# An attention and mixture-of-experts block on one core: VectorE's output sum and its statistics become two steps, one head apart

## The chip, the core and the metric

The kernel is one program on one core of a Trainium2 chip. Its time is device time in microseconds (us), from one launch. TensorE is called PE here, its weight loads PEld, VectorE DVE, ScalarE ACT, GpSimd POOL and SyncE SP, as in the profile.

## The reference

```python
# x: 8 batches x 256 tokens x 256 features
x = x + _layernorm(attn(_layernorm(x)))     # latent attention, 16 heads of 16, softmax over 256 keys, output product wo, bias bo
x = x + _layernorm(ffn(_layernorm(x)))      # 8 experts, top 1, and a shared expert
...
scores = jnp.einsum('bqhd,bkhd->bhqk', q, k) / np.sqrt(hd)
probs = jax.nn.softmax(scores, axis=-1)
a = jnp.einsum('bhqk,bkhd->bqhd', probs, v).reshape(bs, sl, nh * hd)
return _lin(a, wo, bo)
```

`_layernorm` subtracts the mean over the 256 features and divides by the square root of the variance plus 1e-5. The part that the change touches is the tail of the attention of one batch: the sum of the output product and its bias, its normalization, the sum with x, and the statistics of the second normalization, the one before the experts.

## The kernel before

The batches go through eight slots of 16 heads each. Every engine has its own hand-written program, in which a table called `order` says what is done behind which head; engines meet only at semaphores. In slot b the heads of batch b are computed: at head h PE makes the transposed scores (L1623), ACT takes their exponential (L884), and behind every fourth head PE multiplies a group of four heads with v (L1603). Beside that run steps of other batches. A step named with SM, `sm_scores` and `sm_max`, belongs to batch b+1: PE makes the scores of a pair of heads (L1564) into one of two banks in turn, and DVE takes their negated maximum per query (`nmax`, L1098). PE may start the pair u only when the maxima up to u-2 are done, because there are only two banks. Steps with A work on batch b+2, with B on batch b+3, and the tail of the attention (D) on batch b-1 and its second part (E) on b-2. Within a head the maximum comes first and the listed steps behind it.

The D steps form a chain over two engines. DVE adds product and bias (`d_wo`, L1118, semaphore `y_ready`), takes mean and variance (`bn_stats`, `bn_aggr`, L1002, L1006, and L1122 for `var_at`). POOL raises the variance to the power -1/2 (D_power, L644, `rstd_at`). DVE normalizes (D_yn, L1128, two instructions). POOL adds x (D_x1, L684, `x1_ready`). DVE takes the statistics of that sum (D_stats, `stats_ff`, ending in L1136, `var_ff`). POOL takes the power again (D_power2, L644, `rstd`). In the next slot, behind the second head, DVE normalizes for the experts (E_xn2, L1145), and PE transposes that behind the fourth head (E_xn2T, L1430).

POOL has one more task at the beginning of a slot. P_M1 (`m_split`, L672 to L678, four small instructions) splits the second half of the maxima of the slot's own batch into three bfloat16 parts. It stands in POOL's program directly behind D_power2. PE turns the parts behind the third head (M1, L1584), and everything on PE behind M1 waits in line: the products for the keys and queries (L1502), the next heads, and E_xn2T. The rotary step of DVE (A_T, L1054) stands before E_xn2 and is waited for by the products at L1502. A primed name below (u0', h2') is a pair or head of the next slot; heads are counted from 0.

The last slot has lists of its own. In slot 7 the steps for batch 6 and the ones for batch 7 follow each other without maxima between them. The tail of batch 5 ends there: E_xn2 comes behind head 0 on DVE, E_xn2T behind head 2 on PE; behind head 3 comes D_avT0 (L1430), which needs a copy by ACT (D_o1, L877).

Semaphores order all of it:

```python
pe.wait_ge(sm["sm_max"], NH if (b, u) == (1, 0) else NH * b + u - 1)   # PE, a pair of scores
pe.wait_ge(sm["m_parts"], 8 * b + 4 * half + 4)                        # PE, M0 and M1
order = {0: ("P_M1",), 2: ("B_power",), 8: ("A_kres", "M0",),          # POOL
         9: ("A_qres",), 10: ("A_klow",), 11: ("A_qlow",), 12: ("D_power",), 13: ("D_x1",),
         15: ("D_power2",)}
```

Of the kernel before, what the change touches and what calls it, by code (L numbers as in the profile page):

```python
# [116 lines left out]
def program(nc, x, const, w_down, w_q, w_kv, w_rope, w_out, w_router, bias_col, bias_v, bias_o,  # L117
# [6 lines left out]
    with ExitStack() as ctx:  # L124
# [145 lines left out]
        def two(t):  # L270
            return t[:, :].rearrange("p (a c) -> p a c", a=2)
# [39 lines left out]
        def counted(value):  # L311

            return not isinstance(value, int) or value > 0
# [65 lines left out]
        def play(steps, text):  # L379

            for word in text.split():
                name, n = word.split(":")
                steps[name](int(n), int(n) % 2)
# [18 lines left out]
        def run_attention(eng, head, steps, order, last, behind=lambda *_: None):  # L402

            for n, names in PROLOGUE:
                for name in names.split():
                    if name[0] == "S":
                        steps["SM"](0, 0, int(name[1:]))  # L410
                    elif name in steps:
                        steps[name](n, n % 2)
            for b in range(B):
                run_slot(b, b % 2, head, steps, order, last, behind)

        def nothing(*_):
            return None
# [551 lines left out]
        def _(dve):  # L969
# [29 lines left out]
            def ln_head(name, b, tiles, stat, mean_var, var_ap, n):  # L999

                for t in range(n):
                    dve.bn_stats(stat[:, t, :], tiles(t)).then_inc(sm[f"{name}_stats"], 1)  # L1002
                dve.wait_ge(sm[f"{name}_stats"], n * (b + 1))
                dve.sem_inc(sm["passed"], 1)
                for t in range(n):
                    dve.bn_aggr(mean_var(t), stat[:, t, :]).then_inc(sm[f"{name}_aggr"], 1)  # L1006
                dve.wait_ge(sm[f"{name}_aggr"], n * (b + 1))
# [49 lines left out]
            def third_q(m):  # L1057

                def f(b, par):
                    if b != 2:  # L1060
                        return
                    dve.wait_ge(sm["qk_ps"], 3)
                    dve.wait_ge(sm["ql"], 2)
                    dve.wait_ge(sm["q_sb"], 4)
                    dve.tensor_scalar(qf[:, m, :], two(w1)[:, m, :], bcol[:, 2 + m:3 + m], None, ALU.add
                                      ).then_inc(sm["q_sb"], 1)
                return f

            def first_k(m):
                def f(b, par):  # L1070
                    dve.wait_ge(sm["hqk_ps"], 1)
                    for dst, col in ((kh_even, C_EVEN), (kh_odd, C_ODD)):
                        dve.scalar_tensor_tensor(dst[:, m, :], two(st_bank[0])[:, m, :], bcol[:, 14 + m:15 + m],
                                                 cst[:, col:col + 1].to_broadcast([P, S]), ALU.add, ALU.mult
                                                 ).then_inc(sm["hk_sb"], 1)
                return f
# [24 lines left out]
            def divide(t):  # L1101
                def f(b, par):
                    dve.wait_ge(sm["avT_ps"], 2 * b + t + 1)
                    o = w2[:, :].rearrange("p (h c) -> p h c", c=2 * HD)
                    dve.reciprocal(rec[:, :], o[:, :, HD]).then_inc(sm["rec_ready"], 1)
                    dve.wait_ge(sm["rec_ready"], 2 * b + t + 1)
                    if counted(b):
                        dve.wait_ge(sm["aT_ps"], b)
                    dve.tensor_tensor(a_sb[:, t, :].rearrange("p (h c) -> p h c", c=HD), o[:, :, 0:HD],
                                      rec[:, :].unsqueeze(2).to_broadcast([P, NH, HD]), ALU.mult  # L1110
                                      ).then_inc(sm["a_ready"], 1)
                return f

            def d_wo(b, par):
                dve.wait_ge(sm["wo_ps"], b + 1)
                if counted(b):
                    dve.wait_ge(sm["x1_ready"], b)
                dve.tensor_tensor(y_sb[:, :, :], two(w2), bo_sb[:, :].unsqueeze(1).to_broadcast([P, TB, D]),  # L1118
                                  ALU.add).then_inc(sm["y_ready"], 1)
                dve.wait_ge(sm["y_ready"], b + 1)  # L1120
                ln_head("at", b, lambda t: y_sb[:, t, :], stats["at"], lambda t: mv["at"][:, t, :], None, TB)
                dve.tensor_scalar(var["at"][:, :], mv["at"][:, :, 1], EPS, None, ALU.add  # L1122
                                  ).then_inc(sm["at_var"], 1)
# [25 lines left out]
            def d_router(b, par):  # L1149
# [4 lines left out]
            steps = {  # L1154
                "O_rows": ones, "A_ones": ones_and_sums, "A_kv": keys_sum, "A_T": rope, "A_ev0": third_q(0), "A_ev1": third_q(1),
                "H_k0": first_k(0), "H_k1": first_k(1), "B_stats": a_stats, "B_norm": a_norm, "F_stats": first_stats, "F_norm": first_norm, "N_v": v_add, "SM": sm_max,
                "D_div0": divide(0), "D_div1": divide(1), "D_y": d_wo, "D_yn": d_yn, "D_stats": d_stats,
                "E_xn2": d_xn2, "E_router": d_router}
            order = {1: ("A_T", "E_xn2"), 2: ("B_stats",), 3: ("B_norm",), 5: ("E_router",),
                     6: ("D_div0",), 8: ("D_div1",), 9: ("N_v",), 11: ("D_y",),  # L1160
                     12: ("D_yn",), 14: ("D_stats",)}


            done = [0]
# [145 lines left out]
            def unit_copy(seq, n, side):  # L1310
# [3 lines left out]
            steps.update({"O": one_hots, "g": gains, "c": scaled, "p": ranks_of_tokens, "l": low_one_hots,  # L1314
                          "n": expert_places, "m": tile_one_hots, "r": tile_rows, "e": tile_experts, "q": way_back,
                          "h": hidden})
            last = {0: "E_xn2:5", 3: "D_div0:6 D_div1:6", 6: "E_router:5 O:0 D_y:6 D_yn:6 p:0 g:0 c:0 c:1 D_stats:6 c:2 c:3",
                    13: "E_xn2:6"}

            def tile_first(seq, p):  # L1320
# [2 lines left out]

            steps["w"] = tile_first
            run_attention(dve, nothing, steps, order, last)
            play(steps, "D_div0:7 c:4 c:5 E_router:6 D_div1:7 h:0 c:6 c:7 c:8 c:9 D_y:7 h:1 D_yn:7 D_stats:7 h:2 E_xn2:7"
                        " E_router:7 O:1 c:10 c:11 h:3 g:1 c:12 c:13 c:14 c:15 p:1 n:0 h:4 m:0 h:5 l:0 l:1 l:2 l:3 e:0 h:6 r:0 q:0"
                        " h:7 w:8 w:9 h:8")

# [627 lines left out]
```

## Time and profile before

| | |
|---|---|
| time, median of 3 runs | 426.26 us (424.71 to 427.06) |
| the profiled execution | 424.66 us, its span 422.8 us |
| PE busy, of the span | 399.0 us, 94% |
| PEld | 300.2 us, 71% |
| DVE | 272.9 us, 65% |
| ACT | 207.3 us, 49% |
| POOL | 130.6 us, 31% |

The busy shares are means over the whole span. Slots 1 to 4 take 23.4 us each; the times at which an instruction starts, and what ended the idle time before it, are given by the timeline. The end of a PE instruction is modelled, so its start is the safer number.

### The profile page before, as it was taken

What the parts mean: (1) busy time and instruction counts of PE and PEld (TensorE: products, weight loads), DVE (VectorE), ACT (ScalarE), POOL (GpSimd) and SP (SyncE); (2) the same over time, 40 slices, a digit from 0 to 9 for tenths busy, and PEclk for the clock granted to TensorE, in tenths of its full rate; (3) what the DMA queues carried; (4) which work ended last, traced back from release to release, by engine and by line L of the source; (5) the groups of instructions that cost most, each with busy time, mean ns of one, the idle gap of its engine ahead of it and who ended that gap; (6) DMA issues with size and microseconds to landing.
All of it is one profiled execution on the core that took longest, in us unless ns stands there. A gap on an engine that the chain in (4) does not pass through costs nothing.

```text
span 422.8 us, 9481 instructions
## 1 busy us (share of the span) xinstructions
PE 399.0 (94%) x3411; PEld 300.2 (71%) x3411; DVE 272.9 (65%) x632; ACT 207.3 (49%) x381; POOL 130.6 (31%) x185
## 2 busy tenths in 40 slices
PE   8998999999999999797989999999999999999991
PEld 8765557676767776463768999999994444588991
DVE  5665677978878777865675694222226898725876
ACT  1745748585776667545551213344447767311110
POOL 2424515344251615303402002221112220026873
PEclk9999999999999999998999999999999999999998
DMA  7845235373635546450147750011111111124342
GB/s 251 212 119 150 58 94 184 91 225 95 220 85 163 150 111 193 102 175 12 43 144 229 224 177 26 27 50 51 52 50 51 40 47 32 51 59 123 106 127 74
DMA packets 50772, 47.29 MB, mean 112 GB/s; under 512 B 5350, under 2 KB 45542, under 8 KB 50726
## 3 DMA queue, kind: packets, MB, share of 16 engines
q1 hardware_dynamic: 44795, 38.31, 30.8%
q0 software_dynamic: 1632, 4.46, 3.8%
q10 hardware_dynamic: 4299, 3.92, 2.8%
q8 instruction: 28, 0.46, 0.5%
q14 instruction: 18, 0.15, 0.1%
HBM read 25.19 MB, written 8.65 MB: 80 GB/s over the span
## 4 chain that ended last, share of the span: by engine, by line
PE 73%; DVE 13%; issue 4%; POOL 3%; ACT 3%; DMA 2%; another core or an unknown queue 1%; DVEq 0%; ACTq 0%; POOLq 0%
PE bank L1426 32%; PE bank L1754 7%; PE bank L1430 6%; PE bank L1603 6%; PE bank L1623 6%; PE bank L1564 5%; PE bank L1779 3%; DVE nmax L1098 2%; PE bank L1502 2%; PE bank L1439 2%; PE bank L1550 2%; PE bank L1492 1%; DVE wall L1128 1%; DVE stacks L1396 1%; DVE stats_at L1002 1%
## 5 line engine op out<-in xcount | busy, mean ns | idle before, releaser
L1098 DVE TENSOR_REDUCE nmax<-bank 128x2 f32<-128x512 f32 x112 | 74.2, 686 | 27.3 <-PE bank L1564 26.7
L1426 PE MATMUL bank<-stacks,wall 128*128 128x128 f32 x512 | 61.9, 276 | 0.9 <-ACT stacks L920 0.4
L1426 PEld LDWEIGHTS bank<-stacks,wall 128*128 128x128 f32 x512 | 60.0, 192 | 3.5 <-issue 2.4
L1304 DVE TENSOR_TENSOR stacks<-stacks,bank 128x512 f32<-128x512 f32 x34 | 23.3, 686 | 51.9 <-PE bank L1426 47.3
L884 ACT ACTIVATE pv<-bank 128x512 f32<-128x512 f32 x64 | 38.3, 603 | 35.2 <-PE bank L1623 34.3
L920 ACT ACTIVATE stacks<-bank 128x512 f32<-128x512 f32 x34 | 20.3, 597 | 65.3 <-PE bank L1426 38.9
L884 ACT ACTIVATE wall<-bank 128x512 f32<-128x512 f32 x64 | 38.3, 606 | 25.2 <-PE bank L1623 25.1
L1623 PE MATMUL bank<-stacks 99*128 99x256 bf16 x256 | 49.2, 276 | 1.4 <-ACT wall L884 0.9
L1426 PE MATMUL bank<-wall,stacks 128*128 128x256 f32 (+1 forms) x208 | 49.5, 381 | 0.8 <-DVE stacks L1304 0.8
L1564 PE MATMUL bank<-stacks 96*128 96x256 bf16 x224 | 42.3, 273 | 6.6 <-DVE nmax L1098 6.5
L716 POOL DMA_INDIRECT stacks<-x_sc,row_i x18 | 20.3, 1126 | 89.2 <-PE bank L1430 70.1
L1426 PEld LDWEIGHTS bank<-wall,stacks 128*128 128x128 f32 x208 | 37.5, 190 | 5.3 <-DVE stacks L1304 1.2
L1623 PEld LDWEIGHTS bank<-stacks 99*128 99x128 bf16 x256 | 21.6, 100 | 23.5 <-issue 12.4
L1426 PEld LDWEIGHTS bank<-stacks,pv 128*128 128x128 f32 x320 | 37.2, 192 | 1.2 <-ACT stacks L914 0.7
L1426 PE MATMUL bank<-stacks,pv 128*128 128x128 f32 x320 | 37.4, 275 | 0.5 <-ACT stacks L914 0.5
L1754 PE MATMUL bank<-wall,stacks 128*32 x64 | 30.1, 595 | 0.5 <-ACT wdo_sb L933 0.5
L1564 PEld LDWEIGHTS bank<-stacks 96*128 96x128 bf16 x224 | 20.3, 97 | 13.9 <-DVE nmax L1098 11.3
L656 POOL TENSOR_TENSOR wall<-wall,low_sb 128x512 f32<-128x512 f32 x14 | 16.1, 1159 | 38.2 <-ACT low_sb L850 38.2
L731 POOL DMA_INDIRECT pv<-y_exp,back_i x16 | 16.0, 1001 | 33.8 <-DMA y_exp<-stacks 29.7
L1430 PE MATMUL bank<-cst,wall 128*128 128x128 f32 x160 | 24.0, 276 | 1.1 <-ACT wall L877 0.5
L1430 PEld LDWEIGHTS bank<-cst,wall 128*128 128x128 f32 x160 | 17.8, 140 | 4.7 <-issue 1.5
L1312 DVE COPY pv<-wall 128x1024 f32 x24 | 16.7, 695 | 4.3 <-PE bank L1779 1.7
(213 smaller groups left out, 798.4 us busy)
## 6 DMA issues: line engine op xcount, KB each, us to landing
stacks<-low_sb SPq DMA_DIRECT2D x144, 64.0 KB, 2.0
wall<-gate_up SPq DMA_DIRECT2D x8, 1024.0 KB, 5.4
wall<-down SPq DMA_DIRECT2D x8, 512.0 KB, 6.7
y_exp<-stacks ACTq DMA_DIRECT2D x18, 128.0 KB, 1.7
x_tok<-wall SPq DMA_DIRECT2D x8, 256.0 KB, 2.5
stacks<-x_tok SPq DMA_DIRECT2D x16, 128.0 KB
out<-stacks SPq DMA_DIRECT2D x8, 256.0 KB
stacks<-low_sb SPq DMA_DIRECT2D x12, 128.0 KB, 2.4
```

Of the source, the lines that this page charges most:

```text
L716: pool.indirect_dma_start(out=xl[:, par, :], out_offset=None, in_=x_sc, in_offset=bass.IndirectOffsetOnAxis(ap=row_i[:, s - R0:s - R0 + 1] ...
L884: act.activation(probs[h // QUAD % 2][:, h % QUAD, :], st_bank[h % 2][:, :], ACT.Exp, scale=SCALE).then_inc(sm["exp_done"], 1)
L920: act.activation(sg, fg[:, :], ACT.Silu).then_inc(sm["sg_sb"], 1)
L1098: dve.tensor_reduce(nmax[:, half, qt, 2 * pair:2 * pair + 2], two(sm_bank[u % 2]), AX.X, ALU.max, negate=True).then_inc(sm["sm_max"], 1)
L1304: dve.tensor_tensor(to, sg, fu[:, :], ALU.mult).then_inc(sm["h_sb"], 1)
L1312: dve.tensor_copy(to, of).then_inc(sm[("gate_dve", "up_dve", "down_dve")[side]], 1)
L1426: last = pe.matmul(out_ap, lhsT, rhs, start=(n == 0), stop=(n == len(pairs) - 1))
L1430: return pe.transpose(out_ap, in_ap, ident)
L1564: last = pe.matmul(two(sm_bank[u % 2])[:, c, :], stacks[0:ROWS, par, 0, place(h), P * qt:P * qt + P], stacks[0:ROWS, par, 1, place(h), :], ...
L1603: last = pe.matmul(two(av_bank)[32 * c:32 * c + 32, g % 2, :], v_aug[:, par, k, QUAD * g + c, :], probs[g % 2][:, c, S * k:S * k + S], sta ...
L1623: last = pe.matmul(two(st_bank[h % 2])[:, k, :], stacks[0:MROWS, par, 1, place(h), P * k:P * k + P], stacks[0:MROWS, par, 0, place(h), :], ...
L1754: last = pe.matmul((fg, fu)[r][U * n:U * n + U, :], xT[:, p, P * k + U * n:P * k + U * n + U], w, start=(k == 0), stop=(k == KT - 1))
```

## The change

`d_wo` is split: the sum with the bias stays behind head 11 (the twelfth), and the statistics of it become a step of their own, `d_ystats` or D_ys, behind head 12. The normalization D_yn moves from head 12 to 13 and the second statistics D_stats from head 14 to 15. In the lists of slot 7 and behind it, D_ys stands directly behind D_y, so the order of work there is the same as before.

```diff
             def d_wo(b, par):
...
                 dve.tensor_tensor(y_sb[:, :, :], two(w2), bo_sb[:, :].unsqueeze(1).to_broadcast([P, TB, D]),
                                   ALU.add).then_inc(sm["y_ready"], 1)
+
+            def d_ystats(b, par):
                 dve.wait_ge(sm["y_ready"], b + 1)
                 ln_head("at", b, lambda t: y_sb[:, t, :], stats["at"], lambda t: mv["at"][:, t, :], None, TB)
                 dve.tensor_scalar(var["at"][:, :], mv["at"][:, :, 1], EPS, None, ALU.add
...
-                     6: ("D_div0",), 8: ("D_div1",), 9: ("N_v",), 11: ("D_y",),
-                     12: ("D_yn",), 14: ("D_stats",)}
+                     6: ("D_div0",), 8: ("D_div1",), 9: ("N_v",), 11: ("D_y",), 12: ("D_ys",),
+                     13: ("D_yn",), 15: ("D_stats",)}
```

This is DVE's program from the output sum in slot 2 to the beginning of slot 3, before the change (BN_STATS of `stats_at` and `stats_ff` are the two statistics, `nmax` the maxima):

```order
L1118 TENSOR_TENSOR wall<-bank,bo_sb 128x512
L1002 BN_STATS stats_at<-wall 128x6 x2
L1006 BN_AGGR mv_at<-stats_at 128x2 x2
L1122 TENSOR_SCALAR var_at<-mv_at 128x2
L1098 TENSOR_REDUCE nmax<-bank 128x2
L1128 SCALAR_TENSOR_TENSOR wall<-wall,mv_at,rstd_at 128x256 x2
L1098 TENSOR_REDUCE nmax<-bank 128x2 x2
L1002 BN_STATS stats_ff<-x_sb 128x6 x2
L1006 BN_AGGR mv<-stats_ff 128x2 x2
L1136 TENSOR_SCALAR var_ff<-mv 128x2
L1098 TENSOR_REDUCE nmax<-bank 128x2 x3
L1054 SCALAR_TENSOR_TENSOR rope_t<-bank,bcol,cst 128x256
```

And the same place with the change, whose line numbers behind L1118 are higher by two:

```order
L1118 TENSOR_TENSOR wall<-bank,bo_sb 128x512
L1098 TENSOR_REDUCE nmax<-bank 128x2
L1002 BN_STATS stats_at<-wall 128x6 x2
L1006 BN_AGGR mv_at<-stats_at 128x2 x2
L1124 TENSOR_SCALAR var_at<-mv_at 128x2
L1098 TENSOR_REDUCE nmax<-bank 128x2
L1130 SCALAR_TENSOR_TENSOR wall<-wall,mv_at,rstd_at 128x256 x2
L1098 TENSOR_REDUCE nmax<-bank 128x2 x2
L1002 BN_STATS stats_ff<-x_sb 128x6 x2
L1006 BN_AGGR mv<-stats_ff 128x2 x2
L1138 TENSOR_SCALAR var_ff<-mv 128x2
L1098 TENSOR_REDUCE nmax<-bank 128x2 x2
```

Each of the three blocks stands behind one more maximum than before; the number of instructions is the same. POOL's program is not changed. At the same place it reads, in both kernels (two powers, the sum with x between them, then the four instructions of P_M1):

```order
L644 TENSOR_TENSOR rstd_at<-var_at,neg_half 128x2
L684 TENSOR_TENSOR x_sb<-x_sb,wall 128x512
L644 TENSOR_TENSOR rstd<-var_ff,neg_half 128x2
L672 CAST mparts<-nmax 128x2x8
L674 TENSOR_TENSOR nres<-nmax,mparts 128x16
L676 CAST mparts<-nres 128x2x8
L678 TENSOR_TENSOR mparts<-nres,mparts 128x2x8
```

Nothing moved there, nor on PE, ACT and SP.

## Rows read from the trace of the kernel before

**Rows 1.** The page: the chain that ended last, by engine.

```profile
PE 73%; DVE 13%; issue 4%; POOL 3%; ACT 3%; DMA 2%; another core or an unknown queue 1%; DVEq 0%; ACTq 0%; POOLq 0%
```

**Rows 2.** Waits: us in total, times, longest us.

```profile
PE bank L1564 <- DVE nmax L1098: 6.5, 13, 1.1
```

**Rows 3.** Timeline of DVE, end of slot 3: start us, us, instruction, [idle before].

```profile
120.15 0.68 DVE L1118 TENSOR_TENSOR wall<-bank,bo_sb 128x512 f32<-128x512 f32 x1
120.86 0.75 DVE L1002 BATCH_NORM_STATS2 stats_at<-wall 128x6 f32<-128x256 f32 x2
...
122.12 0.69 DVE L1098 TENSOR_REDUCE nmax<-bank 128x2 f32<-128x512 f32 x1
123.03 0.88 DVE L1128 SCALAR_TENSOR_TENSOR wall<-wall,mv_at,rstd_at 128x256 f32<-128x256 f32 x2 [0.22 <-POOL rstd_at L644]
123.83 1.28 DVE L1098 TENSOR_REDUCE nmax<-bank 128x2 f32<-128x512 f32 x2
125.29 0.75 DVE L1002 BATCH_NORM_STATS2 stats_ff<-x_sb 128x6 f32<-128x256 f32 x2 [0.18 <-POOL x_sb L684]
...
126.55 1.99 DVE L1098 TENSOR_REDUCE nmax<-bank 128x2 f32<-128x512 f32 x3
128.46 0.47 DVE L1054 SCALAR_TENSOR_TENSOR rope_t<-bank,bcol,cst 128x256 f32<-128x256 f32 x1
128.85 0.87 DVE L1145 SCALAR_TENSOR_TENSOR wall<-x_sb,mv,rstd 128x256 f32<-128x256 f32 x2
```

**Rows 4.** Timeline of PE, the same stretch: u12, u14, h15, u15, M1.

```profile
120.67 0.38 PE L1564 MATMUL bank<-stacks 96*128 96x256 bf16 x2
...
123.69 0.38 PE L1564 MATMUL bank<-stacks 96*128 96x256 bf16 x2
123.91 0.38 PE L1623 MATMUL bank<-stacks 99*128 99x256 bf16 x2
124.57 0.39 PE L1564 MATMUL bank<-stacks 96*128 96x256 bf16 x2 [0.28 <-DVE nmax L1098]
...
129.05 0.28 PE L1584 MATMUL bank<-idb,mparts 128*24 128x128 bf16 x2
```

**Rows 5.** Timeline of POOL, the same stretch: D_x1, D_power2, P_M1's first and last.

```profile
123.99 1.27 POOL L684 TENSOR_TENSOR x_sb<-x_sb,wall 128x512 f32<-128x512 f32 x1 [1.00 <-DVE wall L1128]
126.72 0.71 POOL L644 TENSOR_TENSOR rstd<-var_ff,neg_half 128x2 f32<-128x2 f32 x1 [1.46 <-DVE var_ff L1136]
127.38 0.20 POOL L672 CAST mparts<-nmax 128x16 bf16<-128x16 f32 x1
...
128.22 0.22 POOL L678 TENSOR_TENSOR mparts<-nres,mparts 128x16 bf16<-128x16 f32 x1
```

**Rows 6.** Timeline, slot 5 to 6: D_stats, E_xn2, M1 and E_xn2T.

```profile
172.01 0.75 DVE L1002 BATCH_NORM_STATS2 stats_ff<-x_sb 128x6 f32<-128x256 f32 x2 [0.18 <-POOL x_sb L684]
...
175.07 0.87 DVE L1145 SCALAR_TENSOR_TENSOR wall<-x_sb,mv,rstd 128x256 f32<-128x256 f32 x2
175.21 0.28 PE L1584 MATMUL bank<-idb,mparts 128*24 128x128 bf16 x2 [0.21 <-POOL mparts L678]
...
176.05 0.41 PE L1430 MATMUL bank<-cst,wall 128*128 128x128 f32 x2
```

**Rows 7.** Timeline, start of slot 7: E_xn2, two of P_M1's, E_xn2T, D_avT0.

```profile
195.69 0.88 DVE L1145 SCALAR_TENSOR_TENSOR wall<-x_sb,mv,rstd 128x256 f32<-128x256 f32 x2 [0.23 <-POOL rstd L644]
195.88 0.36 POOL L674 TENSOR_TENSOR nres<-nmax,mparts 128x16 f32<-128x16 f32 x1
196.31 0.31 POOL L676 CAST mparts<-nres 128x16 bf16<-128x16 f32 x1
...
197.42 0.60 PE L1430 MATMUL bank<-cst,wall 128*128 128x128 f32 x4
...
198.76 0.44 PE L1430 MATMUL bank<-cst,wall 128*128 128x128 f32 x2 [0.52 <-ACT wall L877]
```

**Rows 8.** Windows: us, busy us (instructions) of PE, PEld, DVE, ACT, POOL; PEclk, DMA.

```profile
193.80:197.30 3.50, 3.50 (x29) 1.15 (x22) 2.36 (x8) 1.09 (x2) 1.75 (x5) 0.51 0.00 0
```

More of the change, by code:

```diff
@@ L1156, in _ @@
                 "H_k0": first_k(0), "H_k1": first_k(1), "B_stats": a_stats, "B_norm": a_norm, "F_stats": first_stats, "F_norm": first_norm, "N_v": v_add, "SM": sm_max,
-                "D_div0": divide(0), "D_div1": divide(1), "D_y": d_wo, "D_yn": d_yn, "D_stats": d_stats,
+                "D_div0": divide(0), "D_div1": divide(1), "D_y": d_wo, "D_ys": d_ystats, "D_yn": d_yn, "D_stats": d_stats,
                 "E_xn2": d_xn2, "E_router": d_router}
             order = {1: ("A_T", "E_xn2"), 2: ("B_stats",), 3: ("B_norm",), 5: ("E_router",),
-                     6: ("D_div0",), 8: ("D_div1",), 9: ("N_v",), 11: ("D_y",),
-                     12: ("D_yn",), 14: ("D_stats",)}
+                     6: ("D_div0",), 8: ("D_div1",), 9: ("N_v",), 11: ("D_y",), 12: ("D_ys",),
+                     13: ("D_yn",), 15: ("D_stats",)}
             done = [0]
@@ L1316, in _ @@
                           "h": hidden})
-            last = {0: "E_xn2:5", 3: "D_div0:6 D_div1:6", 6: "E_router:5 O:0 D_y:6 D_yn:6 p:0 g:0 c:0 c:1 D_stats:6 c:2 c:3",
+            last = {0: "E_xn2:5", 3: "D_div0:6 D_div1:6", 6: "E_router:5 O:0 D_y:6 D_ys:6 D_yn:6 p:0 g:0 c:0 c:1 D_stats:6 c:2 c:3",
                     13: "E_xn2:6"}
@@ L1325, in _ @@
             run_attention(dve, nothing, steps, order, last)
-            play(steps, "D_div0:7 c:4 c:5 E_router:6 D_div1:7 h:0 c:6 c:7 c:8 c:9 D_y:7 h:1 D_yn:7 D_stats:7 h:2 E_xn2:7"
+            play(steps, "D_div0:7 c:4 c:5 E_router:6 D_div1:7 h:0 c:6 c:7 c:8 c:9 D_y:7 D_ys:7 h:1 D_yn:7 D_stats:7 h:2 E_xn2:7"
                         " E_router:7 O:1 c:10 c:11 h:3 g:1 c:12 c:13 c:14 c:15 p:1 n:0 h:4 m:0 h:5 l:0 l:1 l:2 l:3 e:0 h:6 r:0 q:0"
```

## Prediction

> **What bounds the kernel now.** The first view is the page's chain of work that ended last: 73% of it is PE and 13% DVE [rows 1]. The bound is PE's own program, and DVE sets the time only where PE must wait for it. The second view, the waits, says where: PE's score pairs wait for DVE's maxima 13 times, 6.5 us in all [rows 2]. The third is the timeline around the edited steps. In slot 3 DVE does the output sum at 120.15 and statistics from 120.86; the maximum of u12 starts only at 122.12, although its scores were made at 120.67 [rows 3, 4]. So DVE is late, the maximum of u13 starts at 123.83, and PE's pair u15 starts at 124.57 [rows 3, 4]. From u14 to h15 PE needs 0.22 us; had u15 followed h15 like that, it would have started at 124.13. The stall is 0.44 us. The pattern stands in slots 1 to 4, four times, 23.4 us apart. Slots 5 and 6 have less work for PE beside the heads and longer waits.
>
> The row that decides this change is one that hardly waits now. M1 on PE (129.05) needs POOL's P_M1, which stands behind D_power2 and so behind DVE's D_stats [rows 4, 5]. In slot 6 PE did wait there: M1 at 175.21 came 3.20 us after D_stats had started at 172.01 [rows 6]. With the same 3.20, slot 3's D_stats at 125.29 would allow M1 at 128.49 [rows 3]. It started at 129.05, so its slack is 0.56 us, and no more.
>
> **The change, step by step, in slots 1 to 4** (times of slot 3). No instruction is added or removed; the price lies in what is late.
>
> 1. The maximum of u12 no longer stands behind the statistics. It is free when PE's pair ends, 120.67 + 0.38 = 121.05 [rows 4], say 121.09. Two maxima take 1.28 and one 0.68, so the next instruction starts 0.60 behind a maximum [rows 3]: the statistics start at 121.69 instead of 120.86, 0.83 late.
> 2. From the statistics to D_yn takes 2.17 us whoever stands between (120.86 to 123.03, with the wait for POOL's power in it), from D_yn to D_stats 2.26 (123.03 to 125.29, with POOL's 1.27 us sum in it) [rows 3, 5]. D_yn comes at 123.86 and D_stats at 126.12. The maxima of u14 and u15 fit in before: D_yn takes 0.80 on DVE (123.03 to 123.83), they end at 124.66 + 1.28 = 125.94.
> 3. The maximum of u13 follows the statistics 1.26 later (120.86 to 122.12), at 122.95, where it was at 123.83 [rows 3]. The release of u15 is 0.74 behind it (123.83 to 124.57) [rows 3, 4], 123.69, so the 0.44 us stall of PE goes.
> 4. D_power2 and P_M1 move with D_stats. M1 can start at 126.12 + 3.20 = 129.32, while PE, 0.44 ahead, is there at 128.61. It waits 0.71 us and ends 0.27 us later than before. The gain of step 3 is swallowed whole.
> 5. P_M1 now also meets other work. Its last instruction starts 2.93 us behind D_stats (125.29 to 128.22) [rows 3, 5], at 129.05. DVE: u0' at 126.12 + 1.26 = 127.38, u1' at 127.98, the rotary step 0.60 later at 128.58, and E_xn2 0.39 behind that (128.46 to 128.85), at 128.97. Before, POOL's four instructions had maxima beside them. The one place where they lie beside E_xn2 is slot 7: there L674 took 0.36 us instead of the 0.22 of L678, a like instruction, and L676 0.31 instead of the 0.20 of L672, a like one [rows 5, 7], 0.25 us together. The bounds are 0 (the last instruction slips in before E_xn2, 0.08 us decide) and 0.25. I take nearly the upper one, 0.24, since E_xn2 starts first and the row shows the same pair of instructions. M1 comes at 129.56, 0.51 late. The rotary step, done by 129.05, is in time for the products behind M1.
>
> Rule of the Trainium skill for step 5: "SBUF — State Buffer" says of the port pair that VectorE and GpSimd share that a VectorE instruction with two SBUF inputs and a GpSimd instruction that reads SBUF exclude each other, the later one waiting until the first is done. By that rule POOL would wait out E_xn2's first half to 129.45 and finish some 0.2 later, so M1 would be 0.65 late in each slot and the sum 0.6 us higher; by the row of slot 7 it is 0.51. The trace agrees in kind: POOL's short instructions grew there and not beside maxima.
>
> Nothing later in these slots gives it back: DVE has caught up by the middle of a slot and PE is the bound again. Four slots: 4 x 0.51 = 2.04 us; by the lower bound 1.1.
>
> **Slot 5 to 6.** D_stats moves by the same 0.83, to 172.84. M1 would come at 176.04, and with 0.25 for E_xn2 beside P_M1 at 176.29. Behind M1 stand a head, a pair and then E_xn2T: six matmuls at 0.11 (half of 0.22), 0.66 us, 176.95. Before, E_xn2T started at 176.05, which was 0.98 behind E_xn2's start at 175.07 [rows 6]; that is not what it waits for now (E_xn2 at 172.84 + 1.26 + 1.20 = 175.30). Cost 0.90 us, with the lower bound of step 5 0.65. The earlier u13 and u14 of slot 5 help nothing, since PE then waits for M1.
>
> **Slot 6 to 7.** E_xn2 moves from 195.69 to 196.52, and E_xn2T can start 0.98 later, 197.50, against 197.42 [rows 6, 7]: 0.08 late. But D_avT0 at 198.76 waited for ACT's copy, which follows the third head on PE [rows 7], and PE ran that stretch at a granted clock of 0.51, the lower of its two levels, 1.2 GHz [rows 8]. The maxima come earlier in slot 6, as in step 3, so PE reaches the third head earlier, and D_avT0 can follow E_xn2T by its 0.66: 198.16. That is 0.6 us gained, if the executions compared had that slow stretch; without it there is a loss of 0.3 instead.
>
> Behind slot 7 the order is the same. The sum is 2.04 + 0.90 - 0.60 = **+2.3 us** on the profiled 424.66, or 427.0. The median of the runs is 1.6 us above the profiled execution, so I put it on 426.26: **428.6 us**.
>
> **The rivals.**
>
> *The stall of PE is all that counts.* If M1 had slack for the 0.83 us, PE would keep 4 x 0.44 = 1.8 us, lose 0.2 at slot 6 (the maximum of u0' there is later), and gain 0.6 in slot 7: -2.1 us, 424.1. For it speaks that the wait for maxima is the largest that PE has in these slots, against it the 0.56 us of slack. It decides when slack exceeds 0.83.
>
> *The port costs nothing.* Only step 4 holds: 1.1 + 0.65 - 0.6 = +1.2 us, 427.4.
>
> *A new stretch at the lower clock.* In slot 6 PE would wait for the maximum of u0' (172.84 + 1.26 + 0.74 = 174.84) and then for M1 until 176.29, with one pair of scores between them. The stretch at 1.2 GHz in slot 7 came behind two waits of up to 1.1 us [rows 2, 8]. 3.4 us at half clock hold 1.7 us of work, so it costs up to 1.7 us more, about 430.0. Against it: the waits before 176 in the trace now did not bring one. The Trainium skill, "TensorE: Matmul & The Clock Gate", Part 1, says that activity holds the clock up and idle time lets it fall to half; the trace agrees, as the fall follows the waits of slot 6.
>
> *It is a wash:* the two waits trade places and the rest of the program hides a few tenths, 426.3 to 427.
>
> **How the numbers follow.** A difference under 0.5%, 2.1 us, can't be told from none here. The forecast has 0.42; being 2.3 us it is slower in 0.26 and same in 0.16. The port that costs nothing has 0.19, all same. The lower clock has 0.24, slower. The stall alone 0.07, faster in 0.05 and same in 0.02, and the wash 0.08, same. That is faster 0.05, same 0.45, slower 0.50. The range runs from 426.6, just below the case without the port, to 430.4, which takes in most of the lower clock; the cases left out are the stall alone and part of the wash.
>
> **What the profile would show.** Step 3: no idle time before L1564 at u15 in slots 1 to 4. Step 4: M1 (L1586 then) waits for POOL's mparts in slots 2 to 5, 0.7 to 1.0 us, and the slot grows from 23.4 to 23.6 or 23.9. Step 5: L680, P_M1's last instruction, takes over 0.3 us. I am wrong if M1 shows no wait, if D_stats starts less than 0.56 later against PE's pair u12, or if the loss in slot 6 is given back before slot 7.

## The result

The kernel with the change takes 431.69 us, the median of six runs (429.61 to 433.84), the kernel before 425.97 us on the same chip (424.71 to 427.06). The ratio on record is 1.0145, with a 95% interval of 1.0113 to 1.0178; it isn't quite the quotient of the medians, which differ by 5.7 us or 1.3%. The forecast was 428.6 us with a range to 430.4. On another chip the ratio was 1.0171 [1.0133, 1.0210]. The profiled execution took 431.2 us (424.66 before) and its span is 429.4 us (422.8).

The page after: the first line of its chain of work that ended last. POOL has 7% of it, where it had 3% [rows 1].

```profile
PE 70%; DVE 12%; POOL 7%; issue 5%; ACT 3%; DMA 2%; another core or an unknown queue 1%; DVEq 0%; ACTq 0%; POOLq 0%
```

The waits after: us in total, times, longest us.

```profile
PE bank L1586 <- POOL mparts L678: 3.7, 6, 0.9
PE bank L1566 <- DVE nmax L1098: 3.7, 7, 1.1
PEld bank L1432 <- DVE wall L1147: 2.9, 2, 2.6
```

The wait for DVE's maxima fell from 6.5 to 3.7 us and from 13 times to 7 [rows 2]. Four of the six that went are the stall of step 3, 0.27 or 0.28 us each by this view, so 1.1 of the 2.8 us; the rest went in slots 5 and 6. M1 (L1586 now) has a wait of 3.7 us in its place, and there is a new wait of E_xn2T (L1432).

Slot 3 to 4, to be laid beside [rows 3 to 5]. Timeline of DVE: output sum, a maximum, statistics; normalization; second statistics; rotary step and E_xn2.

```profile
121.36 0.68 DVE L1118 TENSOR_TENSOR wall<-bank,bo_sb 128x512 f32<-128x512 f32 x1
122.30 0.69 DVE L1098 TENSOR_REDUCE nmax<-bank 128x2 f32<-128x512 f32 x1 [0.26 <-PE bank L1566]
122.90 0.74 DVE L1002 BATCH_NORM_STATS2 stats_at<-wall 128x6 f32<-128x256 f32 x2
...
127.33 0.75 DVE L1002 BATCH_NORM_STATS2 stats_ff<-x_sb 128x6 f32<-128x256 f32 x2 [0.19 <-POOL x_sb L684]
...
129.78 0.47 DVE L1054 SCALAR_TENSOR_TENSOR rope_t<-bank,bcol,cst 128x256 f32<-128x256 f32 x1
130.17 0.87 DVE L1147 SCALAR_TENSOR_TENSOR wall<-x_sb,mv,rstd 128x256 f32<-128x256 f32 x2
```

Timeline of POOL, the same stretch: D_power2, then the four instructions of P_M1.

```profile
128.75 0.70 POOL L644 TENSOR_TENSOR rstd<-var_ff,neg_half 128x2 f32<-128x2 f32 x1 [1.46 <-DVE var_ff L1138]
129.41 0.20 POOL L672 CAST mparts<-nmax 128x16 bf16<-128x16 f32 x1
...
129.97 0.20 POOL L676 CAST mparts<-nres 128x16 bf16<-128x16 f32 x1
130.25 0.48 POOL L678 TENSOR_TENSOR mparts<-nres,mparts 128x16 bf16<-128x16 f32 x1
```

Timeline of PE: h15 and u15, and M1.

```profile
125.11 0.38 PE L1625 MATMUL bank<-stacks 99*128 99x256 bf16 x2
125.33 0.38 PE L1566 MATMUL bank<-stacks 96*128 96x256 bf16 x2
...
130.78 0.28 PE L1586 MATMUL bank<-idb,mparts 128*24 128x128 bf16 x2 [0.69 <-POOL mparts L678]
```

The pair u15 follows h15 without idle time. From the output sum the second statistics start after 5.97 us (127.33 - 121.36), where it was 5.14 (125.29 - 120.15) [rows 3], and M1 after 9.42, where it was 8.90 [rows 3, 4]. So D_stats is 0.83 late and M1 0.52.

Where the rest went shows in the windows from one output sum to the next, slot 5 to 6 and slot 6 to 7. The columns are those of [rows 8]: PEclk is the third from the end. Before:

```profile
166.87:188.38 21.51, 18.55 (x176) 11.93 (x168) 16.53 (x39) 11.68 (x22) 4.29 (x11) 1.00 0.49 146
188.38:206.12 17.74, 14.77 (x126) 8.56 (x119) 10.19 (x32) 9.11 (x18) 5.56 (x8) 0.90 0.10 32
```

After: first the two stretches in which the granted clock is 0.50 (1.2 GHz), then the same two intervals.

```profile
177.15:183.98 6.83, 5.94 (x35) 3.08 (x36) 2.91 (x6) 2.36 (x5) 1.10 (x5) 0.50 0.50 131
204.46:207.87 3.41, 3.14 (x22) 1.71 (x24) 1.32 (x4) 1.94 (x5) 0.00 (x0) 0.50 0.40 126
169.12:193.99 24.87, 21.04 (x176) 12.98 (x168) 16.76 (x39) 11.79 (x22) 4.54 (x11) 0.86 0.43 129
193.99:212.31 18.32, 14.59 (x126) 8.78 (x119) 10.19 (x31) 9.12 (x18) 5.55 (x8) 0.91 0.10 31
```

From slot 5 to 6 PE has the same 176 matmuls and needs 3.36 us more. The kernel before ran slot 5 to 6 at the full clock; this one spends 6.83 us of it at half. Timeline of PE as the clock falls, in slot 6 and in slot 7:

```profile
172.65 0.39 PE L1566 MATMUL bank<-stacks 96*128 96x256 bf16 x2 [0.79 <-DVE nmax L1098]
...
174.88 0.39 PE L1566 MATMUL bank<-stacks 96*128 96x256 bf16 x2 [0.51 <-DMA stacks<-low_sb]
...
177.07 0.57 PE L1566 MATMUL bank<-stacks 96*128 96x256 bf16 x2 [1.14 <-DVE nmax L1098]
178.53 0.39 PE L1586 MATMUL bank<-idb,mparts 128*24 128x128 bf16 x2 [0.89 <-POOL mparts L678]
...
180.67 1.94 PE L1605 MATMUL bank<-wall,pv 128*32 128x256 f32 x16
...
203.06 0.66 PE L1432 MATMUL bank<-cst,wall 128*128 128x128 f32 x4 [2.27 <-DVE wall L1147]
...
203.77 0.60 PE L1432 MATMUL bank<-cst,wall 128*128 128x128 f32 x4
```

In slot 6 waits of 0.79, 0.51 and 1.14 us follow each other, and the clock falls 0.1 us behind the last of them. The wait of 0.89 us for M1 comes when it has fallen. The sixteen matmuls at L1605 take 1.94 us, which are 1.07 at the full clock. In slot 7 the clock falls 1.4 us behind the wait of 2.27. Until then slot 7 goes as forecast: D_avT0 starts 9.78 us behind the output sum (203.77), where it was 10.38 (198.76 - 188.38) [rows 7], the 0.60 us that were to be gained.

From the first to the seventh output sum the account is this, in us (starts of L1118 in the two timelines, 73.43 to 206.12 and 73.62 to 212.31):

| | before | after | difference | forecast |
|---|---|---|---|---|
| four slots | 93.44 | 95.50 | +2.06 | +2.04 |
| slot 5 to 6 | 21.51 | 24.87 | +3.36 | +0.90 |
| slot 6 to 7 | 17.74 | 18.32 | +0.58 | -0.60 |
| together | 132.69 | 138.69 | +6.00 | +2.34 |

### The profile page after: what moved, and what is told of

Read it like the earlier page. It is cut to its first block, busy times and chain, and to the rows that moved or that the text cites. A ratio compares the mean times of both kernels' runs of the same rounds, so it can differ in the third digit from the quotient of the medians.

```text
span 429.4 us, 9481 instructions
## 1 busy us (share of the span) xinstructions
PE 400.9 (93%) x3411; PEld 301.8 (70%) x3411; DVE 273.8 (64%) x632; ACT 207.8 (48%) x381; POOL 131.8 (31%) x185
## 4 chain that ended last, share of the span: by engine, by line
PE 70%; DVE 12%; POOL 7%; issue 5%; ACT 3%; DMA 2%; another core or an unknown queue 1%; DVEq 0%; ACTq 0%; POOLq 0%
PE bank L1428 31%; PE bank L1756 7%; PE bank L1432 6%; PE bank L1605 6%; PE bank L1625 5%; PE bank L1566 4%; PE bank L1781 3%; DVE nmax L1098 2%; POOL x_sb L684 2%; PE bank L1504 2%; PE bank L1441 2%; PE bank L1552 1%; DVE stacks L1398 1%; DVE wall L1130 1%; POOL rstd_at L644 1%
## 5 line engine op out<-in xcount | busy, mean ns | idle before, releaser
L1432 PE MATMUL bank<-cst,wall 128*128 128x128 f32 x160 | 24.9, 284 | 2.7 <-DVE wall L1147 2.3
L1432 PEld LDWEIGHTS bank<-cst,wall 128*128 128x128 f32 x160 | 18.5, 144 | 6.2 <-DVE wall L1147 2.9
```

The costliest lines, as they stand in the source:

```text
L1432: return pe.transpose(out_ap, in_ap, ident)
```

## The experiments

Two theories. **A:** the loss is what the prediction worked out, P_M1 late behind D_power2 and beside E_xn2, and E_xn2 late. **B:** on top of that, PE's new waits bring stretches at half clock (the expectations call this the clock theory). Each kernel is compared with the kernel before on its own chip, since the medians of the kernel before go from 423.3 to 426.8 us from one set of runs to another. The intervals between output sums, the first four as one mean, are from each run's timeline.

| kernel | ratio, 95% interval | slots 1 to 4 | 5 to 6 | 6 to 7 | stretches at 0.5 in the attention |
|---|---|---|---|---|---|
| before | 1 | 23.36 | 21.51 | 17.74 | slot 7 |
| the change | 1.0145 [1.0113, 1.0178] | 23.87 | 24.87 | 18.32 | slots 6 (two in a row), 7 |
| the change, again | 1.0171 [1.0133, 1.0210] | 23.87 | 23.95 | 18.27 | slots 6, 7 |
| slots 1 to 4 alone | 1.0073 [1.0047, 1.0098] | 23.88 | 22.34 | 16.26 | slot 6 |
| slots 5 and 6 alone | 1.0090 [1.0058, 1.0121] | 23.36 | 25.11 | 17.08 | slot 6 (two) |
| E_xn2 one maximum later | 1.0083 [1.0051, 1.0114] | 23.62 | 23.67 | 18.25 | slots 6, 7 |
| P_M1 ahead of D_power2 | 1.0046 [1.0028, 1.0063] | 23.22 | 22.83 | 18.27 | slots 6, 7 |
| and rotary step earlier | 1.0058 [1.0026, 1.0090] | 23.21 | 23.22 | 18.21 | slots 6, 7 |
| before, P_M1 first | 1.0089 [1.0056, 1.0122] | 23.36 | 23.39 | 18.92 | slots 6 (two), 7 |
| before, D_stats later | 1.0037 [1.0007, 1.0066] | 23.36 | 23.67 | 18.80 | slots 6, 7 (two) |
| the change, filled | 1.0069 [1.0035, 1.0104] | 23.87 | 22.58 | 17.07 | none |
| the same, again | 1.0009 [0.9984, 1.0034] | 23.88 | 22.58 | 17.09 | none |
| slot 6 filled | 1.0056 [1.0031, 1.0081] | 23.88 | 22.58 | 18.27 | slot 7 |
| slot 7 filled | 1.0131 [1.0078, 1.0183] | 23.88 | 24.88 | 17.08 | slot 6 (two) |
| before, filled | 0.9918 [0.9887, 0.9949] | 23.36 | 21.51 | 16.27 | none |
| P_M1 first, filled | 0.9938 [0.9914, 0.9962] | 23.22 | 21.69 | 17.09 | none |
| slots 1 to 4, P_M1 first, filled | 0.9986 [0.9960, 1.0011] | 23.23 | 22.20 | 17.86 | none |

"Filled" kernels have idle matmuls, described below. The last column leaves out what comes later: every profile, the one of the kernel before too, has a stretch at half clock at its end, from 418 to 427 us on. Three profiles, the filled change (first run), D_stats later, and the rotary step earlier, have one more at 392, far behind the attention, which nothing here explains.

**P_M1 ahead of D_power2.** The change, with POOL's two tasks swapped; PE's and DVE's programs are the same.

```diff
-            order = {0: ("P_M1",), ...
+            order = {0: ("P_M1", "E_power2"), ...   # E_power2: D_power2 for the batch before
-                     15: ("D_power2",)}
```

> The changed kernel with one more edit, on POOL alone: D_power2 goes behind P_M1 (into the next slot), so that the split of the maxima no longer stands behind the second statistics. Theory: M1 is late only through this queue. Then PE's wait at M1 in slots 2 to 5 goes, the slots shrink from 23.87 to about 23.2 us (the products at the rotary step are then bound by DVE's rotary step, 0.28 us late, so not the whole 0.44 comes back), no stretch at the lower clock follows slot 5, and the time is 424 to 426 us. Rival: it is the later maxima and norms on DVE themselves that PE waits for; then the slots stay at 23.7 to 23.9 and the time at 430 or more.

Slots 1 to 4 fell from 23.87 to 23.22 us, below the kernel before. Timeline of POOL in slot 3 to 4:

```profile
126.46 0.19 POOL L672 CAST mparts<-nmax 128x16 bf16<-128x16 f32 x1
...
127.29 0.22 POOL L678 TENSOR_TENSOR mparts<-nres,mparts 128x16 bf16<-128x16 f32 x1
127.97 0.70 POOL L644 TENSOR_TENSOR rstd<-var_ff,neg_half 128x2 f32<-128x2 f32 x1 [0.47 <-DVE var_ff L1138]
```

P_M1 no longer waits for the statistics, its last instruction is back at 0.22 us, and M1 starts without idle time. That is step 4 of the prediction: the wait for M1 is what takes the gain. The kernel is still 0.46% slower than before, so slots 1 to 4 aren't the whole. That no stretch would follow slot 5 was a miss: there is one in slot 6 and one in slot 7.

**And the rotary step one head earlier.** The same, and A_T behind head 0 on DVE.

```diff
-            order = {1: ("A_T", "E_xn2"), ...
+            order = {0: ("A_T",), 1: ("E_xn2",), ...
```

> The changed kernel, P_M1 ahead of D_power2, and DVE's rotary step one maximum earlier (behind head 0). Theory: both waits that took the place of the removed one are gone, the slots shrink by the whole 0.44 us to 22.9, and the time goes to 423 to 424.5 us, under both kernels. Rival: another wait takes their place (the maximum of u1 or u3 of the next slot, moved by the rotary step): 23.2 us or more.

A miss: 23.21, not 22.9. In PE's timeline h0' waits for a transfer:

```profile
126.63 0.39 PE L1625 MATMUL bank<-stacks 99*128 99x256 bf16 x2 [0.15 <-DMA stacks<-mT]
```

The row is of the kernel with both edits. It comes 5.5 us behind the output sum, 0.23 earlier than in the kernel before, and that is as early as the rows of maxima land. So of the 0.44 us that the prediction's first rival hands back, at most 0.23 could come, and 0.15 did (23.36 - 23.21).

**The change in slots 1 to 4 alone, and in slots 5 and 6 alone.** The steps of DVE stand in the old or the new place by batch.

```diff
+            def placed(new, *fs):
+                def f(b, par):
+                    if (b in (0, 1, 2, 3)) == new:    # the other kernel: (4, 5)
...
```

> The change in slots 1 to 4 alone, the order of before in slots 5 and 6. Theory: each of the four slots takes 0.51 us more, 23.87, and nothing else moves: 428.0 us, ratio 1.005. Rival: the loss beyond 2.3 us comes from these slots too (later stretches at the lower clock, transfers met at another time): 429 to 432.

> The change in slots 5 and 6 alone. Theory: slots 1 to 4 stay at 23.36, M1 of slot 6 comes 1.07 us late, and PE's two long waits there bring the lower clock; 429 to 430 us, ratio 1.007 to 1.010. Rival: the clock plays no part and only the waits count: +0.9 and -0.6 us or +0.3, that is 426.3 to 427.2.

The slots do as they should, 23.88 in the one and 23.36 in the other. But the two parts cost 0.7% (0.5% was expected) and 0.9%, and the second holds two slots only. The first has a stretch at half clock in slot 6, where its order of work is the old one and PE's waits are those of the kernel before. Timeline of PE there, and the window of the stretch:

```profile
172.02 0.39 PE L1576 MATMUL bank<-stacks 96*128 96x256 bf16 x2 [0.84 <-DVE nmax L1098]
...
173.72 0.39 PE L1576 MATMUL bank<-stacks 96*128 96x256 bf16 x2 [1.09 <-DVE nmax L1098]
```

```profile
174.13:177.54 3.41, 3.41 (x24) 1.70 (x25) 2.49 (x8) 0.76 (x2) 1.72 (x6) 0.50 0.39 98
```

In slot 7 neither has a stretch, which gives both orders at the full clock from the output sum of slot 6 to the next. The old order (slots 1 to 4 alone), then the new one:

```profile
191.65:207.91 16.26, 13.24 (x126) 8.25 (x119) 10.20 (x32) 9.12 (x18) 5.55 (x8) 1.00 0.11 35
```

```profile
191.30:208.38 17.08, 13.24 (x126) 8.18 (x119) 10.20 (x31) 9.12 (x18) 5.55 (x8) 1.00 0.11 34
```

**E_xn2 one maximum later.** The change, with E_xn2 behind head 2 on DVE, so that P_M1 has maxima beside it.

```diff
-            order = {1: ("A_T", "E_xn2"), 2: ("B_stats",), ...
+            order = {1: ("A_T",), 2: ("E_xn2", "B_stats",), ...
```

> The changed kernel, with E_xn2 on DVE one head later (behind the maximum of head 2), so that it no longer lies beside P_M1. Theory of the shared port: P_M1's last instruction is back at 0.22 us instead of 0.48, M1 comes 0.26 us earlier, slots of 23.6 us, and four slots give 1.0 us: 430.6 from 431.7. Rival: the 0.48 has another cause (the queue or the semaphores of POOL): it stays, and the slots too.

Slots of 23.62 us: of the 0.51 us per slot 0.25 are E_xn2 beside P_M1, and 0.26 the wait itself. The timeline of POOL has the instruction that took 0.48 us:

```profile
129.84 0.22 POOL L678 TENSOR_TENSOR mparts<-nres,mparts 128x16 bf16<-128x16 f32 x1
```

**The kernel before with one part each.** D_stats alone one head later, and P_M1 alone ahead of D_power2.

```diff
-                     12: ("D_yn",), 14: ("D_stats",)}      # the kernel before
+                     12: ("D_yn",), 15: ("D_stats",)}
```

> The kernel before with D_stats alone one head later. Theory of the slack: D_stats comes 0.42 us late (0.60 for the maximum of u15, less the 0.18 that it waited), under M1's slack of 0.56, so the slots stay at 23.36 and PE waits as before; slot 6 loses 0.4 at most: 426 to 426.8 us. Rival: every delay of D_stats costs its length: 23.8 us a slot, 428 or more.

> The kernel before with POOL's D_power2 behind P_M1. Theory: M1 was not late there, so nothing is gained; the wait of 0.44 us for the maximum stays; the slots stay at 23.36, 425.5 to 427 us. Rival: the queue on POOL already cost something before: faster by 0.5% or more.

Neither moves slots 1 to 4, and both are slower all the same, by 0.4% and 0.9%, where at most 0.2% was expected of either. Both have stretches at half clock that the profile of the kernel before doesn't have, and theory A has no term for them. Part of the loss is work: in slot 6 E_xn2T comes 0.58 us later with D_stats moved and 0.66 with the swap. The two parts weren't taken apart here, since neither kernel was filled.

**Idle matmuls where PE waits.** The change with matmuls of ones into a free bank, 22 and 14 in slot 6 ahead of u2' and M1, 34 in slot 7 ahead of E_xn2T. They keep PE at work in time that it spent waiting, and nothing reads their result.

```diff
+            def fill(slot, n):
...
+                        for _ in range(n):
+                            pe.matmul(w0[:, 0:P], ones_bf[:, :], ones_bf[:, :], start=True, stop=True)
```

> The changed kernel with idle products for PE in the places where it waits in slots 6 and 7: 22 behind head 1 and 14 ahead of M1 in slot 6, 34 ahead of E_xn2T in slot 7 (128x128 bfloat16 of ones into a bank that nothing reads until it is written anew). They compute nothing that is used. Theory: the loss beyond the waits is the clock, which falls after the waits of slot 6; with PE busy there it stays at the higher level, slot 5 to 6 shrinks from 24.87 to about 22.5 us, and the time goes to 428 to 429.5. Rival: the slot is long by its waits alone, and the filling makes it no shorter or even longer: 431 to 433.

> The changed kernel once more, so that it and its version with idle matmuls are timed against the same runs of the kernel before. Both theories expect what was measured first, a ratio near 1.014 (1.011 to 1.018), slots of 23.87 us, and a half-clock stretch in slot 6; the clock theory says that what it has over the filled version of this call is the price of the stretches. If the two come out within 0.2% of each other, the clock is not the second half of the loss.

> The changed kernel with 22 and 14 idle matmuls in slot 6 and 34 in slot 7, which the program needs for nothing, as timed before on another chip (ratio 1.007, slots 23.87, no half-clock stretch in the attention). Clock theory: 0.5 to 0.9% below the changed kernel of this call, since the port and the wait for M1 stay and the stretches go. Rival (the loss is all in the waits, and the stretches only cover idle time): within 0.2% of the changed kernel.

Timed side by side on one chip, the change stood at 432.93 us and its filled version at 426.20, 1.6% apart. PE does 70 matmuls more and is faster. The windows between the output sums of the filled version:

```profile
169.20:191.78 22.58, 20.49 (x212) 13.96 (x204) 16.62 (x38) 11.80 (x22) 4.55 (x11) 1.00 0.47 142
191.78:208.87 17.09, 15.15 (x160) 10.17 (x153) 10.21 (x32) 9.12 (x18) 5.56 (x8) 1.00 0.11 34
```

The order of work that the kernel needs is the same, and the clock is 1.00 in both. M1 of slot 6 starts 9.42 us behind the output sum, as it did without the fill (9.41), so the idle matmuls neither delay nor hasten it. And where a profile without them happened to have no stretch, slots 5 and 6 alone, slot 6 to 7 took 17.08 us, the same as here. So theory B holds: 2.29 us (24.87 - 22.58) and 1.23 us (18.32 - 17.09) are the price of the stretches in the profile of the change.

**Is each stretch local?** One place filled at a time.

> The changed kernel with the 22 and 14 idle matmuls of slot 6 alone. If each half-clock stretch follows the waits just ahead of it, the one of slot 6 goes (from the output sum of slot 5 to that of slot 6 22.6 us instead of 24.0 to 24.9) and the one behind the 2.3 us wait for E_xn2 in slot 7 stays (18.3 us from there to the next sum); time halfway between the changed kernel and its filled version. If the stretches have one common cause, both go or both stay.

> The changed kernel with the 34 idle matmuls ahead of E_xn2T in slot 7 alone. Local theory: the stretch in slot 6 stays (23.9 to 24.9 us), the one in slot 7 goes (17.1). Common cause: both go or both stay.

Windows with slot 6 filled:

```profile
169.94:192.52 22.58, 20.58 (x212) 13.88 (x204) 16.61 (x38) 11.74 (x22) 4.55 (x11) 1.00 0.48 142
192.52:210.79 18.27, 14.74 (x126) 9.23 (x119) 10.20 (x31) 9.23 (x18) 5.56 (x8) 0.91 0.10 31
```

And with slot 7 filled:

```profile
169.50:194.38 24.88, 21.01 (x176) 12.99 (x168) 16.76 (x38) 11.79 (x22) 4.54 (x11) 0.86 0.44 128
194.38:211.46 17.08, 15.14 (x160) 10.16 (x153) 10.20 (x31) 9.12 (x18) 5.55 (x8) 1.00 0.10 34
```

Each fill removes the stretch behind it and leaves the other, to 0.05 us. The stretches are local, and filling the waits ahead of one removes it.

**The kernel before, filled,** with 12 and 16 matmuls ahead of the waits at the ends of slots 5 and 6, 8 in slot 6, and 14 ahead of E_xn2T; **and the change, filled, with P_M1 first.**

> The kernel before with idle matmuls put ahead of its waits for maxima: 12 and 16 behind heads 13 and 14 of slots 5 and 6, 8 behind head 0 of slot 6, 14 ahead of E_xn2T in slot 7. Clock theory: the one stretch of before (193.8 to 197.3) goes, E_xn2T starts 0.98 behind E_xn2, some 0.7 us earlier than now, the step from the output sum of slot 6 to that of slot 7 falls from 17.74 to 16.3 to 17.0, ratio 0.997. The filled version of the change then stands 2.3 to 3.2 us above this one, all of it waits. Rival (a stretch costs nothing because the waits cover it): ratio 1.000. Above 1.002: the idle matmuls delay the heads themselves, and no verdict.

> The change, POOL's P_M1 ahead of D_power2, and idle matmuls: 12 behind head 14 of slots 5 and 6, 18 behind head 1 of slot 6, 34 ahead of E_xn2T in slot 7. If both causes are named rightly (M1's wait behind D_power2, and half-clock stretches behind waits of PE), then with both removed the change keeps its gain: slots 1 to 4 of 23.22, no stretch in slots 6 and 7, 17.1 us from the output sum of slot 6 to that of slot 7, ratio 0.997 (0.994 to 1.000). With a third cause in slots 6 and 7 it stays above 1.002.

The kernel before gains 0.82%, more than the 0.3% expected, and is at 422.82 us; its slot 6 to 7:

```profile
189.30:205.57 16.27, 15.38 (x168) 10.64 (x161) 10.20 (x32) 9.23 (x18) 5.55 (x8) 1.00 0.11 35
```

So its own stretch had cost 1.47 us (17.74 - 16.27; without the fill and without a stretch the old order took 16.26). Against it the filled change is 3.4 us slower in the medians on the same chip, and 3.96 by the sums of the profiles, where 2.3 to 3.2 were expected: 2.07 in four slots, 1.07 in slot 5 to 6, 0.82 in slot 6 to 7. With P_M1 first it has 0.14 us less than before in each of slots 1 to 4, but the 0.82 stays, as E_xn2 comes that much later (8.14 us behind the output sum for 7.31).

**The change where it pays.** New order in slots 1 to 4 alone, P_M1 first, and the idle matmuls of the kernel before.

> The new order in slots 1 to 4 alone, where it pays once P_M1 stands ahead of D_power2, with that swap in all slots, and the idle matmuls that the kernel before had (12, 16, 8 and 14). By the profiles: 0.14 us less in each of four slots than the kernel before with idle matmuls, 0.8 less than the whole change with them in slot 7, so 130.7 us from the first output sum to the seventh and a ratio of 0.990. If the swap costs in slots 5 and 6 (E_xn2T comes later there), 131.2 and 0.992.

A miss: 0.9986. Timeline of POOL in slot 7:

```profile
196.42 0.20 POOL L672 CAST mparts<-nmax 128x16 bf16<-128x16 f32 x1 [2.04 <-DVE nmax L1098]
...
197.26 0.22 POOL L678 TENSOR_TENSOR mparts<-nres,mparts 128x16 bf16<-128x16 f32 x1
197.44 0.70 POOL L644 TENSOR_TENSOR rstd<-var_ff,neg_half 128x2 f32<-128x2 f32 x1
```

And of DVE and PE, which wait behind it:

```profile
195.60 0.17 DVE L1138 TENSOR_SCALAR var_ff<-mv 128x2 f32<-128x2 f32 x1
198.18 0.88 DVE L1147 SCALAR_TENSOR_TENSOR wall<-x_sb,mv,rstd 128x256 f32<-128x256 f32 x2 [1.82 <-POOL rstd L644]
199.11 0.66 PE L1442 MATMUL bank<-cst,wall 128*128 128x128 f32 x4 [1.38 <-DVE wall L1147]
```

Where D_stats is early, as in these two slots, the swap makes D_power2 wait for maxima that it doesn't need: its variance is ready at 195.77 and it starts at 197.44. E_xn2T comes 1.54 us later in slot 7 than in the filled kernel before (9.84 us behind the output sum for 8.30) and 0.67 later in slot 6 (9.84 for 9.17). Together that is 2.2 of the 2.3 us by which the profile missed the forecast (132.96 us from the first to the seventh output sum, for 130.7). A kernel with the swap only in the slots where the change stands was not run. The lowest ratio of this study is that of the kernel before with idle matmuls, 0.9918 [0.9887, 0.9949]; the interval of the filled change with P_M1 first (0.9938) overlaps it.

## Why the prediction was wrong

The step that failed is the one that put *a new stretch at the lower clock* at nothing in the sum. It was named as a rival, with a chance of 0.24, and left out of the forecast because "the waits before 176 in the trace now did not bring one". Stretches cost 3.52 of the 6.00 us between the output sums, and 3.52 of the 3.66 us by which the sum of +2.34 missed. The trace has 6.83 us at half clock in slot 6, which cost 2.29, and 3.41 in slot 7 behind the 2.27 us wait for E_xn2, which cost 1.23. The rival's price of at most 1.7 us for a stretch of 3.4 held; it had counted one such stretch, where there were three such lengths.

The reason given for leaving it out was one execution. In the profile with the change in slots 1 to 4 alone, the same waits at the same place, 0.84 and 1.09 us in slot 6, had a stretch behind them, and so they had in the kernel before with P_M1 first. So its absence in the trace before showed only that these waits need not bring one, and the longer waits of the change were laid beside a lucky execution.

**Steps 1 to 3** were right: both statistics 0.83 late against the output sum, the stall of 0.44 us gone. What it could be worth was less, 0.23 at most, since h0' meets the landing of the rows of maxima.

**Step 4** named the right wait: with P_M1 first it is gone and the slots take 23.22. Its size agrees by luck only. The 0.71 us were for step 4 alone, and with step 5 the forecast wait was 0.95 (129.56 - 128.61). The trace has 0.69 with both, because PE came to M1 about 0.2 us ahead and not 0.44. How late M1 is doesn't depend on that, and was right: 0.26 us without step 5 (23.62 - 23.36), where 0.27 was forecast.

**Step 5** was right in size, 0.25 us per slot, shown by moving E_xn2 (23.62 against 23.87). It lies in one instruction, L678 (the prediction calls it L680), 0.48 us for 0.22, and not in the two that slot 7 had suggested. Together 0.52 per slot, where 0.51 was forecast. The rule of the Trainium skill, "SBUF — State Buffer", "Who interferes with whom", on the port pair, would have had 0.65. The trace agrees with it in kind: L678 ends at 130.73, just behind the first of the two instructions of E_xn2, which takes 0.47 us from 130.17. In size the row decides, 0.26 us more and not 0.38.

**Slot 5 to 6**, without stretches, cost 1.07 (22.58 - 21.51); 0.90 was forecast. M1 came 1.07 late, as worked out (1.08), and E_xn2T didn't make up the 0.18 that the forecast had allowed. The wait of u0' for the landing of low_sb, 0.51 us, was not seen.

**Slot 6 to 7** gained the 0.60 us of the forecast up to D_avT0, as worked out, and then lost 1.2 us to its own stretch. Filled, it is 0.65 below the kernel before with its stretch (17.09 against 17.74). Where neither has a stretch, the loss is 0.82 and not 0.3: all of E_xn2's delay reaches PE.

Without stretches in the change, then, the sum is 2.06 + 1.07 - 0.65 = +2.5 us, where the forecast had +2.3. That is still against a kernel before with a stretch that cost it 1.47. Between the two orders of work alone the difference is 3.96 us; the stretches add 3.52 and take off 1.47, which makes the 6.0.

**Executions without a profile.** The fill was worth 6.7 us between the medians on one chip, while the profiles (of the change first profiled and its filled version) differ by 3.5 between the output sums. The mean granted clock, on record for every execution, accounts for a part. On that chip the six of the change had 0.981 to 0.988, the twelve of the filled one 0.994 to 0.997. With the two levels of the profiles, 1.00 and 0.50, that is 10 to 16 us at half clock in the one and 3 to 5 in the other, 12 us apart in the medians. A microsecond at half clock cost 0.24 (slots 1 to 4 alone, slot 6) to 0.43 us (the kernel before, slot 7) in the profiles, so by this estimate the clock was worth 2.9 to 5.2 of the 6.7 us. The kernel before had 0.982 to 0.996 there in 26 executions: it, too, has more time at half clock in some executions than in others. The filled change stood at 1.0069 on one chip and at 1.0009 on another; its mean clock had a median of 0.991 on the first and 0.997 on the second, so the fills left more time at half clock there, while its intervals are the same to 0.02 us.

**What stays open.** It isn't shown what decides whether a row of waits brings a stretch. The same pair, 0.84 and 1.1 us, stands in slots 5 and 6 of the kernel before, and the clock fell behind the second pair only. The wait of 2.27 us in slot 7 brought a stretch in the change, and none in the profile with the change in slots 5 and 6 alone.

## What to carry to other kernels

Where PE is near its limit, count each new wait twice: once for its own time, and once for the clock that may fall behind it, which cost 3.5 us here and had cost the kernel before 1.5. That one profile shows no such fall says little, as the next execution may have it. When a step is moved later on one engine, look past the instruction that it frees to the queue of the engine it feeds: POOL's small task P_M1 stood behind D_power2, which had to wait for the moved step, without needing it. And put a few idle matmuls into waits before you compare two orders of work; they show what the orders themselves are worth.

## What the runs showed of the hardware

In the change the granted clock fell to 0.5 behind waits of PE that were never longer than 1.14 us in slot 6 and 2.27 in slot 7. It stayed there for 3.41 us, or for 6.83 though PE was busy 5.94 of them. The same waits were followed by a stretch in some profiles and by none in others. The Trainium skill, "TensorE: Matmul & The Clock Gate", Part 1, says that activity holds the clock up; the trace agrees, since 36 small matmuls in slot 6 kept it at 1.00, and M1 behind them came no later (9.42 us behind the output sum, 9.41 without them).

A POOL instruction on 16 numbers per partition took 0.22 us beside DVE's maxima and 0.48 beside E_xn2, which reads x_sb and rstd in SBUF, in all four slots. It ended 0.09 us behind the first instruction of E_xn2 (130.73 and 130.64); before, in slot 7, L674 with its 0.36 us ended 0.07 behind it (196.24 and 196.17) [rows 7].

Behind the last output sum, where the order of work is the same, these executions differ by 6 us (span less the start of the last sum: 195.9 to 201.9, and up to 200.1 without the stretch at 392). A comparison of two spans can't see a difference of 1 us. The intervals between like instructions can: in all 17 profiles the one from the seventh output sum to the eighth is 18.45 to 18.46 us, and those of slots 1 to 4 of the change are 23.86 to 23.89 in its six profiles, filled or not.
